# Experts' outputs of a mixture-of-experts layer: scatter to two tables in memory in place of a combine on TensorE

## The chip, the cores and the metric

One core of a Trainium2 chip runs the whole program. The metric is the device time of one execution in microseconds (us), lower is better. The three runs before the change have a median of 1986.42 us (1985.71 to 1988.87).

## What is computed

The program is a four-layer model on x of shape (8, 256, 128) float32, that is 2048 tokens of 128 channels. The change touches only the last stage, a mixture of experts. Reduced to what matters:

```python
p = softmax(router(layernorm(x)))             # (2048, 32)
top2 = the two largest of p for each token
for e in range(32):                           # each expert takes at most 80 tokens, by score
    rows = the 80 best-scored tokens that chose e
    h = silu(xe @ up_a[e]) * (xe @ up_b[e])   # 256 wide; plus a shared 128-wide part, times 0.05,
    y = h @ down[e]                           # whose weights two neighbouring experts share
    y = y * score / (sum of the token's two scores)
    moe[rows] += y
x_out = x + gate * moe
```

A token is in at most two experts' rows. Rows with score 0 fill an expert's 80 slots and count nothing.

## The kernel before, in words

Five engines run programs of their own and meet at barriers (`barrier`, L239). The attention and node layers ahead of the last stage take 1694 of 1995 us and are not touched.

The last stage (`moe_sp`, `moe_pool`, `moe_pe`, `moe_act`, `moe_dve`, L1725 to L2073) has three parts.

- Routing. VectorE normalises x into Qf and makes the tokens' statistics, TensorE and ScalarE the router, VectorE the two best experts of each token. SyncE stores the rows (Qf and one over the sum of a token's two scores) to the table s_rows in memory (L1743). Then VectorE takes each expert's 80 best tokens, eight at a time (L2000 to L2003). `slot` holds score and token number of each expert's 80 slots, `sloti` the number as an integer.
- The loop over 32 experts. POOL gathers 80 rows of s_rows into one of four buffers xg (L1764). TensorE transposes them (`turn`, L1811), ScalarE copies the result to xeT (L1901). TensorE multiplies with six 128-column weights (`up`, L1824, 80 columns of xeT each), ScalarE takes SiLU (L1905), VectorE makes the two parts of he (L2019, L2021), TensorE multiplies with the three second weights (`down`, L1835). VectorE scales y (L2035, L2041) and splits it into two parts of the fast matmul format (yb, L2043, L2045). VectorE also builds for each expert a one-hot matrix `sel` of 80 x 2048 (L2028), and TensorE adds y to the tokens' places by eight matmuls of 80 rows and 512 columns (`combine`, L1844); banks 0 to 3 gather all experts' sums. TensorE's order in a step is down(e), up(e+1), turn(e+2), combine(e). A gather waits until yb of four experts before is done (L1763). SyncE loads the weights of two experts (960 KB in four DMAs, L1737) into one of two buffers. First and last four experts are written out; the others are a hardware loop (`Fori`) of four.
- The end. VectorE copies four banks (L2064), TensorE transposes 16 blocks (L832), VectorE adds them, times the gate, onto X (L2070), SyncE stores 1 MB (L2077).

```python
            def step(e, u, par, first=False, left=4):
                down(e, u, par)
                if left > 1:
                    up(e + 1, (u + 1) % 4, ((u + 1) % 4) // 2)
                if left > 2:
                    turn(e + 2, (u + 2) % 4)
                combine(e, u, first, left == 1)
```

Of the kernel before, what the change touches and what calls it, by code (L numbers as in the profile page):

```python
# [140 lines left out]
def flamingo(nc, T, out):  # L141
    with ExitStack() as ctx:
# [1541 lines left out]
        iotaT = V[:, 0:NTOK]  # L1684
# [6 lines left out]
        XG = sb("XG", [P, NT, D + 1], scope=s5)  # L1691
# [4 lines left out]
        xg = sb("xg", [CAP, 4, D + 1], scope=s5)  # L1696
        xeT = sb("xeT", [P, 2, CAP], scope=s5)
        Wup = sb("Wup", [P, 2, 2, 512], scope=s5)
        Wdn = sb("Wdn", [P, 2, 2, 2, D], scope=s5)
        Aup = sb("Aup", [P, 2, 256], scope=s5)  # L1700
        Adn = sb("Adn", [P, 2, D], scope=s5)
        sil = sb("sil", [P, 2, 3, CAP], scope=s5)
        he = sb("he", [P, 2, 3, CAP], scope=s5)
        wsl = sb("wsl", [CAP, 2], scope=s5)
        ye = sb("ye", [CAP, 2, D], scope=s5)
        yb = sb("yb", [CAP, 2, 2, D], F32R, scope=s5)
        with ExitStack() as s6:
            sc = sb("sc", [E, 2, NTOK], scope=s6)
        sel = sb("sel", [CAP, 2, NTOK], F32R, scope=s5)
# [15 lines left out]
        def moe_sp(s):  # L1725
            e = s.eng
            for dst, src in moe_loads():
                e.dma_start(dst, src).then_inc(dma_in, 16)
            s.count("in", 6)

            def load_group(g, par):
                for dst, src in ((Wup[:, par], T["L3_upT"][ds(g, 1)].rearrange("a p e j -> p (a e) j")),
                                 (Wdn[:, par].rearrange("p e k c -> p (e k) c"),
                                  T["L3_downT"][ds(g, 1)].rearrange("a p x c -> p (a x) c")),
                                 (Aup[:, par], T["L3_aupT"][ds(g, 1)].rearrange("a p j -> p (a j)")),
                                 (Adn[:, par], T["L3_adnT"][ds(g, 1)].rearrange("a p j -> p (a j)"))):
# [10 lines left out]
            with e.Fori(0, (G - 2) // 2) as i:
                for par in range(2):

                    e.wait_ge(m_y_full, 2 * (2 * i + par + 1))  # L1750
                    load_group(2 * i + par + 2, par)
            s.barrier()
            s.barrier()

        def moe_pool(g):
# [4 lines left out]
            for k in range(E):  # L1760
                if k >= 4:

                    e.wait_ge(m_yb, 3 * (k - 3))  # L1763
# [3 lines left out]
            g.barrier()  # L1767
            g.barrier()

        def moe_pe(p):  # L1770
# [35 lines left out]
            def turn(e, u):  # L1806

                pe.wait_ge(m_g[u], 4 * (e - u) + 16)
                if not isinstance(e, int) or e >= 1:
                    pe.wait_ge(m_xt_free, e)  # L1810
                pe.transpose(bank[4][:, 0:CAP], xg[:, u, 0:D], ident[0:CAP, 0:CAP]).then_inc(m_xt_full, 1)  # L1811

            def up(e, u, par):

                q = u % 2
                if u % 2 == 0:
                    pe.wait_ge(m_w[par], 16 * (e - 2 * par) + 64)
                pe.wait_ge(m_xt_free, e + 1)
                o = bank[5 + q]

                for k in range(6):
                    w = (Wup[:, par, q, k * P:(k + 1) * P] if k < 2 else Aup[:, par, 0:P] if k == 2 else
                         Wup[:, par, q, (k - 1) * P:k * P] if k < 5 else Aup[:, par, P:2 * P])
                    last = pe.matmul(o[:, k * CAP:(k + 1) * CAP], w, xeT[:, q, :], start=True, stop=True,  # L1824
                                     skip_group_check=True)
                last.then_inc(m_up_full, 1)

            def down(e, u, par):
                q = u % 2
                pe.wait_ge(m_h, 2 * e + 2)  # L1830
                if not isinstance(e, int) or e >= 1:
                    pe.wait_ge(m_yb, 3 * e)
                for k in range(3):
                    w = Wdn[:, par, q, k] if k < 2 else Adn[:, par]
                    last = pe.matmul(bank[7][0:CAP, 0:D], he[:, q, k, :], w, start=(k == 0), stop=(k == 2))  # L1835
                last.then_inc(m_y_full, 1)

            def combine(e, u, first=False, end=False):
                q = u % 2
                pe.wait_ge(m_yb, 3 * e + 3)  # L1840
                pe.wait_ge(m_sel, e + 1)
                for c in range(4):
                    for k in range(2):
                        last = pe.matmul(bank[c][:, :], yb[:, q, k, :], sel[:, q, c * 512:(c + 1) * 512],  # L1844
                                         start=(first and k == 0), stop=(end and k == 1), skip_group_check=True)
                last.then_inc(m_comb, 1)

            def step(e, u, par, first=False, left=4):
                down(e, u, par)
                if left > 1:  # L1850
                    up(e + 1, (u + 1) % 4, ((u + 1) % 4) // 2)
                if left > 2:
                    turn(e + 2, (u + 2) % 4)
                combine(e, u, first, left == 1)
            turn(0, 0)
            up(0, 0, 0)
            turn(1, 1)
            for u in range(4):
                step(u, u, u // 2, first=(u == 0))
            with pe.Fori(1, E // 4 - 1) as i:  # L1860
                for u in range(4):
                    step(4 * i + u, u, u // 2)
            for u in range(4):
                step(E - 4 + u, u, u // 2, left=4 - u)
            p.barrier()
            transposes_pe(p, lambda t: xfT[:, t * P:(t + 1) * P], who="DDDD")
            p.barrier()

        def moe_act(a):
# [26 lines left out]
            def front(e, u):  # L1896
                q = u % 2
                act.wait_ge(m_xt_full, e + 1)
                if not isinstance(e, int) or e >= 2:
                    act.wait_ge(m_up_full, e - 1)  # L1900
                act.copy(xeT[:, q, :], bank[4][:, 0:CAP]).then_inc(m_xt_free, 1)  # L1901
                act.wait_ge(m_up_full, e + 1)
                if not isinstance(e, int) or e >= 2:
                    act.wait_ge(m_h, 2 * e - 2)
                act.activation(sil[:, q], bank[5 + q][:, 0:3 * CAP].rearrange("p (k s) -> p k s", k=3),  # L1905
                               ACT.Silu).then_inc(m_sil, 1)
            for u in range(4):
# [302 lines left out]
```

## Time and profile before

| | |
|---|---|
| median of three runs | 1986.42 us |
| the profiled execution's own time | 1996.73 us |
| its span, first to last instruction | 1994.8 us |
| last stage: first DMA issue of L1728 to the end | 1694.3 to 1994.8 us |
| TensorE busy | 1377.0 us (69%) |
| VectorE busy | 1362.2 us (68%) |
| ScalarE, POOL busy | 752.7 us, 410.0 us |
| granted clock of TensorE, mean | 0.852 of 2.4 GHz |

The profile is of one execution. Its own time is 10 us above the median of the unprofiled runs. Times in the rows count from the span's start. PE is the matmul side of TensorE, PEld its weight loads, DVE is VectorE, ACT ScalarE, SP SyncE; a "q" behind an engine's name marks its sequencer. A float32 matmul shows as two records.

### The profile page before, as it was taken

How to read it: one execution, taken by the hardware profiler on the slowest of the kernel's cores; microseconds unless marked ns; L12 is line 12 of the kernel's file. 1: busy time of each engine (PE TensorE's matmuls, PEld its weight loads, DVE VectorE, ACT ScalarE, POOL GpSimd, SP SyncE). 2: the span in 40 equal slices, each digit the busy share in tenths (PEclk: the TensorE clock that was granted, in tenths of full speed). 3: DMA queues.
4: the chain of work that ended last, by engine and by line, in shares of the span. 5: the costliest groups of instructions: out<-in, count | busy, mean ns of one | idle time of the engine just before them, and what ended most of it. 6: DMA issues, size and time to landing. Idle time of an engine off the chain costs nothing. (4 is left out here: it accounts for less than half of the span.)

```text
span 1994.8 us, 32063 instructions
## 1 busy us (share of the span) xinstructions
PE 1377.0 (69%) x12362; PEld 955.8 (48%) x12362; DVE 1362.2 (68%) x2054; ACT 752.7 (38%) x1092; POOL 410.0 (21%) x588
## 2 busy tenths in 40 slices
PE   0798189999999933888888834299514887120997
PEld 0565156666666621555665522166404454110897
DVE  5564457777777766676777778476587675869565
ACT  1255147667777731333333312145321365100110
POOL 6243232222222100222222200434102100000221
PEclk9898589999999975899999965589757799555899
DMA  2242322222232201000000000222001320110342
GB/s 69 49 68 35 92 81 88 83 89 89 85 91 85 89 24 41 1 1 1 1 1 1 1 11 0 48 60 53 12 0 32 65 50 19 61 21 0 93 146 86
DMA packets 115183, 95.88 MB, mean 48 GB/s; under 512 B 44180, under 2 KB 98516, under 8 KB 114132
## 3 DMA queue, kind: packets, MB, share of 16 engines
q1 hardware_dynamic: 114020, 92.63, 17.5%
q8 instruction: 96, 1.57, 0.3%
q0 software_dynamic: 1024, 1.32, 0.3%
q14 instruction: 43, 0.35, 0.1%
HBM read 33.23 MB, written 3.15 MB: 18 GB/s over the span
## 5 line engine op out<-in xcount | busy, mean ns | idle before, releaser
L586 ACT ACTIVATE Pt<-bank 128x1024 f32<-128x1024 f32 (+1 forms) x384 | 366.1, 953 | 181.0 <-PE bank L530 179.3
L642 DVE TENSOR_REDUCE l0f_Mf<-bank 128x4 f32<-128x1024 f32 x192 | 234.5, 1222 | 108.1 <-PE bank L509 108.0
L550 PE MATMUL bank<-Pt,V 128*32 128x256 f32 (+1 forms) x3072 | 199.0, 378 | 10.1 <-POOL Pt L391 8.9
L1102 POOL TENSOR_TENSOR Psum<-Pt 128x512 f32<-128x512 f32 x64 | 81.1, 1267 | 321.7 <-ACT Pt L1221 321.7
L550 PEld LDWEIGHTS bank<-Pt,V 128*32 128x32 f32 x3072 | 82.2, 112 | 82.8 <-issue 29.4
L832 PE MATMUL bank<-ident,Qf 128*128 128x128 f32 x64 | 14.1, 414 | 154.4 <-SPq L242 91.5
L391 POOL TENSOR_SCALAR_AFFINE_SELECT Pt<-Pt 128x512 f32<-128x512 f32 x128 | 81.5, 637 | 181.0 <-ACT Pt L586 181.0
L1269 DVE RECIPROCAL st<-bank 128x256 f32<-128x256 f32 x64 | 111.9, 1749 | 6.9 <-PE bank L1182 6.8
L1244 DVE TENSOR_TENSOR qk_lo<-bank,qk_hi 128x512 fp32r<-128x512 f32 x64 | 44.1, 689 | 103.2 <-ACT qk_hi L1213 103.2
L530 PE MATMUL bank<-l0f_QK 64*128 64x256 f32 x768 | 97.6, 333 | 19.8 <-DMA l0f_QK<-l0f_NMrow 19.2
L407 POOL CAST parts<-nodes 128x256 fp32r<-128x256 f32 x96 | 38.0, 396 | 305.1 <-PE bank L481 305.1
L642 DVE TENSOR_REDUCE l2x_Mf<-bank 128x4 f32<-128x1024 f32 x64 | 76.8, 1220 | 32.7 <-PE bank L509 32.7
L1764 POOL DMA_INDIRECT xg<-s_rows,sloti x32 | 29.3, 916 | 330.1 <-PEq L242 237.9
L1221 ACT ACTIVATE Pt<-bank 128x1024 f32<-128x1024 f32 x64 | 65.5, 1024 | 77.7 <-PE bank L1165 77.7
L530 PEld LDWEIGHTS bank<-l0f_QK 64*128 64x128 f32 x768 | 57.9, 187 | 73.2 <-ACT Pt L586 34.0
L832 PEld LDWEIGHTS bank<-ident,Qf 128*128 128x128 f32 x64 | 12.9, 224 | 155.3 <-SPq L242 92.2
L1177 PE MATMUL bank<-Pt,V 128*64 128x256 f32 x512 | 70.3, 395 | 19.6 <-DVE AnT L1271 19.6
L509 PE MATMUL bank<-l0f_QK 63*128 63x256 f32 x768 | 78.6, 283 | 5.8 <-DVE l0f_Mf L642 5.8
L1213 ACT CAST qk_hi<-bank 128x512 fp32r<-128x512 f32 x64 | 37.5, 586 | 115.0 <-PE bank L1121 115.0
L1248 DVE TENSOR_REDUCE Mx<-bank 128x4 f32<-128x1024 f32 x64 | 77.8, 1216 | 1.0 <-PE bank L1140 1.0
L590 ACT COPY OT<-bank 128x512 f32<-128x512 f32 x96 | 56.2, 586 | 54.6 <-PE bank L550 54.6
L559 PE MATMUL bank<-ident,OT 128*128 128x128 f32 x384 | 63.3, 289 | 13.0 <-ACT OT L590 5.5
(363 smaller groups left out, 3383.7 us busy)
## 6 DMA issues: line engine op xcount, KB each, us to landing
l0f_QK<-l0f_Z SPq DMA_DIRECT2D x288, 128.0 KB, 2.4
l2x_QK<-l2x_Z SPq DMA_DIRECT2D x96, 128.0 KB
Wup<-in_L_upT SPq DMA_DIRECT2D x16, 512.0 KB, 3.5
l0x_QK<-l0x_Z SPq DMA_DIRECT2D x48, 128.0 KB
Wdn<-in_L_downT SPq DMA_DIRECT2D x16, 256.0 KB, 3.6
Aup<-in_L_aupT SPq DMA_DIRECT2D x16, 128.0 KB, 3.5
l0f_QK<-l0f_NMrow SPq DMA_DIRECT2D x96, 4.0 KB
WeT<-in_L_WeT SPq DMA_DIRECT2D x1, 1280.0 KB
```

Source lines behind the costliest of these rows:

```text
L391: e.affine_select(diagonal, diagonal, [[0, 2], [0, 2], [1, P]], ALU.is_ge, 0.0, base=0, channel_multiplier=-1).then_inc(L.kept, 1)
L509: last = pe.matmul(bank[L.first(j) + x][:, t * S:t * S + w], L.QK[rs, u % L.ring, j, 0, t * P:(t + 1) * P], L.QK[rs, u % L.ring, j, 1, 0:w ...
L530: last = pe.matmul(bank[2 + x][:, t * S:t * S + S - q0], L.QK[rs, u % L.ring, j, 1, t * P:(t + 1) * P], L.QK[rs, u % L.ring, j, 0, q0:S], ...
L550: last = pe.matmul(bank[4][32 * x:32 * x + 32, o + q0:o + S], Va[:, 2 * n + k, 4 * j + x, :], Pp[:, (f + x // 2) % 4, x % 2, k * S:k * S + ...
L559: last = pe.transpose(b[:, (2 * t + k) * P:(2 * t + k + 1) * P], OT[:, k, t * P:(t + 1) * P], ident[:, :])
L586: act.activation(Pp[:, g % 4, :, 0:w], banks[:, 2:4, 0:w], ACT.Exp, scale=L.scale).then_inc(exp_done, 1)
L642: d.tensor_reduce(m, A.rearrange("p h (t k) -> p h t k", t=2), AX, ALU.max).then_inc(max_done, 1)
L1102: e.tensor_tensor(Psum[:, q % 2], Pp[:, q % 4, :, 0:S], Pp[:, q % 4, :, S:2 * S], ALU.add).then_inc(key_sum, 1)
L1177: pe.matmul(y[64 * x:64 * x + 64, 0:S], Vr[:, u % 8, k, 2 * j + x, :], Pp[:, g % 4, x, k * S:(k + 1) * S], start=(k == 0), stop=(k == 1), ...
L1221: act.activation(Pp[:, g % 4], banks[:, 2:4, :], ACT.Exp, scale=float(DH1) ** -0.5).then_inc(l1_exp, 1)
L1248: d.tensor_reduce(m[:, :, 2 * j:2 * j + 2].rearrange("p t h -> p h t"), banks[:, 0:2, :].rearrange("p h (t k) -> p h t k", t=2), AX, ALU.m ...
L1269: d.reciprocal(st1[:], y[:, S:2 * S]).then_inc(pair_done, 1)
```

## The change

Each expert's weighted rows are no longer added on TensorE. Two tables in memory, s_y_even and s_y_odd, have two rows for each token, one for its first and one for its second expert, and 160 rows that nobody reads. Both are filled with zeros at the stage's start (4 MB in two DMAs). VectorE works out a row number for each of the 80 slots (dsti), and POOL scatters ye (80 x 128) by it, into s_y_even for even experts and s_y_odd for odd ones. Scatter k waits for ye(k), and for the landing of scatter k-2 of the same table. Gather k+4 is issued behind scatter k. At the end SyncE waits for all scatters and reads both tables back (4 MB, eight DMAs with pieces of 1 KB), VectorE adds the four parts of each token and adds them times the gate onto X, in four chunks, and SyncE stores each chunk (256 KB).

With it: `combine`, `sel`, `yb`, the copies and transposes of the end go; TensorE's order in a step is turn(e+2), up(e+1), down(e), and down has two banks in turn; the loops of all engines are written out; the weights of two experts are one tensor of 960 KB and one DMA, with nine buffers in place of two, four of them in V; the load of a 1 MB iota goes; rows of s_rows are 130 floats wide in place of 129.

```diff
-        iotaT = V[:, 0:NTOK]
+        NW, WV = 9, 4
+        Wg = sb("Wg", [P, NW - WV, 1920], scope=s5)
...
+        Yl = V[:].rearrange("p (t a b c) -> p t a b c", t=NT, a=2, b=2)
...
         def moe_sp(s):
...
-            load_group(0, 0)
-            load_group(1, 1)
+            for y in ("s_y_even", "s_y_odd"):
+                e.dma_start(T[y][0:2 * NTOK].rearrange("(p r) c -> p (r c)", p=P),
+                            T["c_zero"].to_broadcast([P, 2 * NTOK * D // P])).then_inc(m_zero, 16)
+            for i in range(5):
+                e.dma_start(weights(i), T["L3_experts"][i]).then_inc(m_w[i], 16)
...
+            for i in range(NW, G):
+
+                e.wait_ge(m_y_full, 2 * (i - NW + 1))
+                e.dma_start(weights(i), T["L3_experts"][i]).then_inc(m_w[i % NW], 16)
+            for u in range(4):
+                e.wait_ge(m_put[u], 16 * (E // 4))
+            for c in range(4):
+                for b, y in enumerate(("s_y_even", "s_y_odd")):
+                    e.dma_start(Yl[:, 4 * c:4 * c + 4, b],
+                                T[y][1024 * c:1024 * (c + 1)].rearrange("(t p a) c -> p t a c", p=P, a=2)
+                                ).then_inc(m_fin[c], 16)
+            for c in range(4):
+                e.wait_ge(m_x, c + 1)
+                e.dma_start(out.rearrange("b (t p) c -> p (b t) c", p=P)[:, 4 * c:4 * c + 4],
+                            X[:, 4 * c:4 * c + 4]).then_inc(dma_out, 16)
...
         def moe_pool(g):
...
-            for k in range(E):
-                if k >= 4:
-
-                    e.wait_ge(m_yb, 3 * (k - 3))
+            for k in range(4):
+                gather(k)
+            for k in range(E):
+
+                e.wait_ge(m_rows, 2 * k + 2)
+                if k >= 2:
+                    e.wait_ge(m_put[(k - 2) % 4], 16 * ((k - 2) // 4 + 1))
+                e.indirect_dma_start(out=T["s_y_odd" if k % 2 else "s_y_even"],
+                                     out_offset=bass.IndirectOffsetOnAxis(ap=dsti[:, k % 4:k % 4 + 1], axis=0),
+                                     in_=ye[:, k % 4, :], in_offset=None).then_inc(m_put[k % 4], 16)
+                if k + 4 < E:
+                    gather(k + 4)
...
         def moe_pe(p):
...
+            turn(0)
+            turn(1)
+            up(0)
+            for e in range(E):
+                if e + 2 < E:
+                    turn(e + 2)
+                if e + 1 < E:
+                    up(e + 1)
+                down(e)
...
         def moe_dve(v):
...
+            v.link(d.tensor_scalar(dump[:], dump[:], 2.0, float(2 * NTOK), ALU.mult, ALU.add))
+            d.tensor_scalar(live[:], slot[:, 0], 0.0, None, ALU.is_gt)
+            v.link(d.tensor_scalar(rowS[:], slot[:, 1], 2.0, dump[:], ALU.mult, ALU.subtract))
+            v.link(d.tensor_tensor(rowS[:], rowS[:], live[:], ALU.mult))
+            v.link(d.tensor_scalar(rowS[:], rowS[:], dump[:], None, ALU.add))
...
+                d.scalar_tensor_tensor(out=dsti[:, u:u + 1], in0=xg[:, u, D + 1:D + 2], scalar=iotaE[0:CAP, e:e + 1],
+                                       in1=rowS[:, e:e + 1], op0=ALU.not_equal, op1=ALU.add).then_inc(m_rows, 1)
                 d.wait_ge(m_y_full, e + 1)
...
+                d.tensor_scalar(ye[:, u, :], bank[2 + e % 2][0:CAP, 0:D], xg[:, u, D:D + 1], slot[:, 0, e:e + 1],
+                                ALU.mult, ALU.mult).then_inc(m_rows, 1)
+            front(0)
+            for e in range(E):
+                if e + 1 < E:
+                    front(e + 1)
+                back(e)
...
             for c in range(4):
...
+                d.wait_ge(m_fin[c], 32)
+                two = Yl[:, 4 * c:4 * c + 4]
+                v.link(d.tensor_tensor(two[:, :, 0], two[:, :, 0], two[:, :, 1], ALU.add))
+                v.link(d.tensor_tensor(y, two[:, :, 0, 0], two[:, :, 0, 1], ALU.add))
+                d.scalar_tensor_tensor(out=x, in0=y, scalar=g, in1=x, op0=ALU.mult, op1=ALU.add).then_inc(m_x, 1)
```

How the steps stand on TensorE, in the middle of the loop, before (one step of the written-out experts; Wup, Wdn and Aup, Adn are an expert's own and the shared weights):

```order
L1835 MATMUL bank<-Wdn,he 80x128 x2
L1835 MATMUL bank<-Adn,he 80x128
L1824 MATMUL bank<-xeT,Wup 128x80 x2
L1824 MATMUL bank<-xeT,Aup 128x80
L1824 MATMUL bank<-xeT,Wup 128x80 x2
L1824 MATMUL bank<-xeT,Aup 128x80
L1811 MATMUL bank<-ident,xg 128x80
L1844 MATMUL bank<-sel,yb 128x512 x8
```

and after the change (two steps; Wg is the tile of the weights):

```order
L1834 MATMUL bank<-ident,xg 128x80
L1846 MATMUL bank<-xeT,Wg 128x80 x6
L1858 MATMUL bank<-Wg,he 80x128 x3
L1834 MATMUL bank<-ident,xg 128x80
L1846 MATMUL bank<-xeT,Wg 128x80 x6
L1858 MATMUL bank<-Wg,he 80x128 x3
```

The combine is gone, and the transpose of expert e+2, which waits for its gather, now stands ahead of up(e+1) and down(e).

On POOL, before, the loop is one row:

```order
L1764 DMA xg<-s_rows,sloti 80x129 x32
```

and after the change, from the loop's start:

```order
L1776 DMA xg<-s_rows,sloti 80x130 x4
L1786 DMA s_y_even<-ye,dsti 4256x128
L1776 DMA xg<-s_rows,sloti 80x130
L1786 DMA s_y_odd<-ye,dsti 4256x128
L1776 DMA xg<-s_rows,sloti 80x130
```

Gathers 0 to 3 still stand ahead; from then on each gather is issued behind a scatter that waits for ye.

## Rows read from the trace of the kernel before

**Rows 1.** Windows: length, busy us (count) by engine, granted clock, DMA share, GB/s.
```profile
1675.00:1685.00 10.00, 6.83 (x84) 3.59 (x88) 0.82 (x3) 6.73 (x7) 0.00 (x0) 1.00 0.01 2
1751.50:1755.50 4.00, 4.00 (x31) 4.00 (x30) 0.00 (x0) 1.02 (x1) 0.00 (x0) 0.79 0.00 0
1848.00:1856.00 8.00, 6.79 (x31) 6.58 (x32) 2.59 (x7) 1.94 (x4) 2.09 (x3) 0.50 0.06 13
1856.00:1859.80 3.80, 3.80 (x11) 2.95 (x11) 1.73 (x4) 0.49 (x2) 0.00 (x0) 0.50 0.04 11
1859.80:1863.00 3.20, 3.20 (x18) 3.20 (x16) 0.86 (x3) 0.00 (x0) 0.57 (x1) 0.50 0.22 42
1863.00:1980.00 117.00, 116.52 (x800) 105.06 (x799) 77.12 (x209) 15.13 (x59) 23.87 (x27) 1.00 0.39 126
```

**Rows 2.** Groups by line from 1840 us on: count, busy us, mean ns.
```profile
L1844 PE MATMUL bank<-sel,yb 80*128 80x512 f32 x256 | 68.5, 411 | 1.1 <-DVE yb L2045 1.1
L2028 DVE TENSOR_SCALAR sel<-V,slot 80x2048 fp32r<-80x2048 f32 x32 | 40.8, 1276 | 0.0
```

**Rows 3.** Timeline at 1.2 GHz, the loop's start: start us, us, instruction.
```profile
1853.31 0.98 PEld L1824 LDWEIGHTS bank<-xeT,Wup 128*128 128x128 f32 x4
...
1853.84 0.35 DVE L2041 TENSOR_SCALAR ye<-bank,wsl 80x128 f32<-80x128 f32 x1 [0.47 <-PE bank L1835]
...
1855.79 0.31 PEld L1811 LDWEIGHTS bank<-ident,xg 80*128 80x128 f32 x1
...
1856.25 0.37 ACT L1905 ACTIVATE sil<-bank 128x240 f32<-128x240 f32 x1 [4.59 <-PE bank L1824]
...
1859.64 1.06 PE L1835 MATMUL bank<-Wdn,he 128*80 128x128 f32 x4
```

**Rows 4.** Timeline at 2.4 GHz: one expert's step, and the last ye.
```profile
1971.48 0.53 PEld L1824 LDWEIGHTS bank<-xeT,Wup 128*128 128x128 f32 x4
...
1971.85 0.34 DVE L2041 TENSOR_SCALAR ye<-bank,wsl 80x128 f32<-80x128 f32 x1 [0.44 <-DVE wsl L2035]
...
1972.78 0.18 PEld L1811 LDWEIGHTS bank<-ident,xg 80*128 80x128 f32 x1
...
1973.81 0.23 DVE L2021 SCALAR_TENSOR_TENSOR he<-sil,bank 128x80 f32<-128x80 f32 x1
...
1975.76 0.35 DVE L2041 TENSOR_SCALAR ye<-bank,wsl 80x128 f32<-80x128 f32 x1 [0.46 <-DVE wsl L2035]
...
1979.62 0.35 DVE L2041 TENSOR_SCALAR ye<-bank,wsl 80x128 f32<-80x128 f32 x1 [0.40 <-DVE wsl L2035]
```

**Rows 5.** Timeline: a gather on POOL behind VectorE, and one behind another gather.
```profile
1847.37 0.91 POOL L1764 DMA_INDIRECT xg<-s_rows,sloti  x1 [0.30 <-issue]
...
1854.48 0.29 DVE L2045 TENSOR_TENSOR yb<-ye,yb 80x128 fp32r<-80x128 f32 x1
...
1855.04 0.91 POOL L1764 DMA_INDIRECT xg<-s_rows,sloti  x1 [5.55 <-DVE yb L2045]
```

**Rows 6.** The tile s_rows: its gathers from issue to landing.
```profile
DMA to landing us min/median/max: 2.3/2.6/5.0
```

**Rows 7.** Timeline, the end of the program.
```profile
1986.09 3.16 DVE L2070 SCALAR_TENSOR_TENSOR X<-bank,gates,X 128x512 f32<-128x512 f32 x4 [0.86 <-PE bank L832]
1989.32 0.41 SPq L2077 DMA_DIRECT2D x_out<-X  x1
```

**Rows 8.** Windows over DMAs: 512 B pieces in, weights (pieces of 2 to 4 KB), output (512 B).
```profile
4.00:5.50 1.50, 0.00 (x0) 0.00 (x0) 0.00 (x0) 0.00 (x0) 0.00 (x0) 1.00 1.06 321
1700.00:1705.00 5.00, 0.00 (x0) 0.00 (x0) 4.14 (x4) 0.62 (x1) 0.00 (x0) 0.50 1.01 401
1991.00:1994.00 3.00, 0.00 (x0) 0.00 (x0) 0.00 (x0) 0.00 (x0) 0.00 (x0) 0.50 1.01 284
```

**Rows 9.** Timeline: a wide and a small operation of VectorE.
```profile
1712.16 2.29 DVE L1925 TENSOR_TENSOR O<-Qf,st 128x2048 f32<-128x2048 f32 x1
...
1842.74 0.19 DVE L2004 TENSOR_SCALAR vals<-vals 32x80 f32<-32x80 f32 x1
```

More of the change, by code:

```diff
@@ L1743, in moe_sp @@
             e.dma_start(T["s_rows"].rearrange("(t p) c -> p t c", p=P), XG[:]).then_inc(xg_out, 16)
+            for i in range(5, NW):
+                e.dma_start(weights(i), T["L3_experts"][i]).then_inc(m_w[i], 16)
             e.wait_ge(xg_out, 16)
+            e.wait_ge(m_zero, 32)
             s.barrier()
             s.barrier()
[L1747 to L1752, printed above, removed]
+            for i in range(NW, G):
[12 more added lines that the diff above has]
+                            X[:, 4 * c:4 * c + 4]).then_inc(dma_out, 16)
+            s.count("out", 4)
             s.barrier()
@@ L1818, in up @@
+            def up(e):
+                q, g = e % 2, e // 2
+                w = weights(g)
+                pe.wait_ge(m_w[g % NW], 16 * (g // NW) + 16)
                 pe.wait_ge(m_xt_free, e + 1)
-                o = bank[5 + q]
+                if e >= 2:
+                    pe.wait_ge(m_h, 2 * e - 2)
                 for k in range(6):
[L1822 to L1825, printed above, removed]
+                    o = q * 512 + k * P if k < 2 else 1536 if k == 2 else q * 512 + (k - 1) * P if k < 5 else 1664
+                    last = pe.matmul(bank[5 + q][:, k * CAP:(k + 1) * CAP], w[:, o:o + P], xeT[:, q, :], start=True,
+                                     stop=True, skip_group_check=True)
@@ L1826, in up, with down @@
                 last.then_inc(m_up_full, 1)
-            def down(e, u, par):
-                q = u % 2
+            def down(e):
+                q = e % 2
+                w = weights(e // 2)
                 pe.wait_ge(m_h, 2 * e + 2)
-                if not isinstance(e, int) or e >= 1:
-                    pe.wait_ge(m_yb, 3 * e)
+                if e >= 2:
+                    pe.wait_ge(m_rows, 2 * e - 2)
                 for k in range(3):
-                    w = Wdn[:, par, q, k] if k < 2 else Adn[:, par]
-                    last = pe.matmul(bank[7][0:CAP, 0:D], he[:, q, k, :], w, start=(k == 0), stop=(k == 2))
+                    o = 1024 + q * 256 + k * P if k < 2 else 1792
+                    last = pe.matmul(bank[2 + q][0:CAP, 0:D], he[:, q, k, :], w[:, o:o + P], start=(k == 0),
+                                     stop=(k == 2))
@@ L1836, in down @@
                 last.then_inc(m_y_full, 1)
[L1838 to L1866, printed above, removed]
+            turn(0)
[7 more added lines that the diff above has]
+                down(e)
             p.barrier()
@@ L2047, in step @@
-            def step(e, u, end=False):
-                back(e, u)
-                if not end:
-                    front(e + 1, (u + 1) % 4)
-                    choose(e + 1, (u + 1) % 4)
-            front(0, 0)
-            choose(0, 0)
-            for u in range(4):
-                step(u, u)
-            with d.Fori(1, E // 4 - 1) as i:
-                for u in range(4):
-                    step(4 * i + u, u)
-            for u in range(4):
-                step(E - 4 + u, u, end=(u == 3))
@@ L2073, in moe_dve @@
             v.barrier()
         def finish_sp(s):
-            s.eng.dma_start(out.rearrange("b (t p) c -> p (b t) c", p=P), X[:]).then_inc(dma_out, 16)
-            s.eng.wait_ge(dma_out, 16 * s.count("out", 1))
+            s.eng.wait_ge(dma_out, 16 * s.count("out", 0))
         block = ctx.enter_context(nc.Block())
```

129 lines of the change are left out of this document (49 added, 80 removed).

## The prediction

> **What bounds the kernel now.** First the windows. From 1863 to 1980 us PE is busy 116.52 of 117.00 us at the full clock, VectorE 77 us: the loop is bound by TensorE [rows 1]. Then the groups by line: of that time the combine, L1844, is the largest part, 68.5 us or 2.14 us an expert [rows 2]. Then the timeline, for the pace: ye starts at 1971.85 and 1975.76, so an expert takes 3.91 us; the last ye ends at 1979.97, the first at 1854.19 [rows 3, 4]. The end is serial: behind the last ye come combine, copies, transposes, the addition to X and a store, 14.8 us to the span's end at 1994.8 [rows 4, 7]. The sum below goes against this execution, whose own time, 1996.73 us, is 10.3 us above the median of 1986.42; I carry the difference over to the median. A measurement can tell about 0.2%, 4 us, from no change.
>
> **Ahead of the loop: +1 us.** Four linked small operations and a fifth make the row numbers before POOL may start, at 0.19 us and a gap each [rows 9]: 1.0 us, on the path. The zeros (4.2 MB) and weights (4.9 MB) are asked for at 1694 and on; at the 400 GB/s of the weights' window that is 23 us, even at half of it 46 us, and nobody needs them before the loop, 150 us later [rows 8]. Nothing for them; if the cover were gone it would be seen at the s_rows store. The weights in the loop come nine buffers ahead, also nothing.
>
> **The loop: a new wait.** The combine and `sel` go. What is left on PE for an expert, by the starts of weight loads: at 2.4 GHz up 1.30 us (1971.48 to 1972.78), down and turn 0.8 more, 2.1 together [rows 4]; at 1.2 GHz up 2.48 us (1853.31 to 1855.79), down 1.3 (four of its six records 1.06, less overlap) and turn 0.2, 4.0 together [rows 3]. But PE waits. Gather k+4 stands behind scatter k, scatter k behind ye(k); on PE turn(k+4) stands ahead of up(k+3) and down(k+2), which ye(k+2) needs. So two experts cost one round:
> - ye to POOL's start 0.27 us (1854.77 to 1855.04) [rows 5];
> - the scatter on POOL 0.91 + 0.30 [rows 5]. No row shows a scatter; the gather, 80 pieces of 516 B, is nearest, and I take it. Nothing at all is the lower end, twice it the upper;
> - the gather to its landing 2.6, from 2.3 to 5.0 [rows 6];
> - turn and its start 0.3;
> - up(k+3) to ye(k+2). VectorE makes he(k+3) ahead of ye(k+2). At 2.4 GHz from 1971.48 to 1974.04 for he, then dsti 0.15 and ye 0.35: 3.1 us [rows 4]. At 1.2 GHz up and down take 3.8 on PE, some 0.2 to finish, ye 0.35: 4.4 us [rows 3].
>
> Sums: 7.5 us a pair at 2.4 GHz, 8.8 at 1.2 GHz, or **3.7 and 4.4 us an expert**, against 3.91 now. So the clock decides the sign.
>
> **The clock.** PE begins the loop at 1.2 GHz. From 1848 to 1856 it does turns, ups and downs, is busy 6.79 of 8.00 us, the last three throughout, and the clock stays low; it rises at 1863.0, behind the first combine (1856 to 1859.8), a down and an up [rows 1]. In the router's matmuls, 1751.5 to 1755.5, it falls (0.79 on average) while PE is busy 4.00 of 4.00 us [rows 1]. The new loop consists of just the turns, ups and downs that ran eight microseconds at the low level here, with PE waiting 0.4 us an expert besides. I take it that the clock stays at 1.2 GHz for about two thirds of the loop, and that where it rises, the waits (PE then busy 2.1 of 3.7 us) bring it back down in part. Against that: at 1675 to 1685 it holds 1.00 with PE busy 6.83 of 10 us [rows 1]. The Trainium skill (TensorE: Matmul & The Clock Gate, "What's actually happening") says that the throttled state is the default and that the clock is set by how busy PE has recently been; read as busy time, that rule would raise the clock after the first experts, which is the rival below; the rows from 1848 to 1856 do not agree with that reading.
>
> The loop in numbers: ye(0) moves from 1854.2 to 1857.2 (1.0 ahead, turn(2) and up(1) now before down(0), 2.9, less 0.9 us in which PE stood idle), ye(1) follows at 1861.3 (PE's 4.0). Then 28 experts to ye(29): two thirds at 4.4 and a third at 3.7, 116.7 us: 1978.0. The last two need no gather: 4.5 us. ye(31) ends at 1982.5, against 1980.0: **+2.5 us**. All at 1.2 GHz: 1861.3 + 123.2 + 5.2 = 1989.7, +9.7. All at 2.4 GHz from ye(1) on: 1861.3 + 103.6 + 2.9 = 1967.8, -12.2.
>
> **The end: +7 us.** From the last ye: POOL 0.3, the scatter's landing 2.6 (as a gather), SyncE's issue to first data 1.1. Then 4.2 MB in pieces of 1 KB: the windows show 321/1.06 = 303 GB/s for 512 B and some 400 for larger pieces [rows 8]; I take 365, 11.5 us, from 10.5 to 13.9. A receipt 0.4. VectorE then adds the last chunk: half of 2.29, a quarter and a bit (0.69), and 0.75: 2.7 us with links [rows 7, 9]; the other chunks go beside the reads. SyncE's last store, 256 KB: issue to data 1.0, 0.9 at 284 GB/s, landing and end 0.9: 2.8 us [rows 7, 8]. Together 21.4, against 14.8: **+6.6 us**, from +5 to +10. The Trainium skill (DMA: Bandwidth & Descriptors, "Anatomy of one DMA") fits 2.0 us plus bytes over 436 GB/s; by that the reads would take 11.6 us with their start, 1 us less than my 12.6 to the same point.
>
> **Sum:** +2.5 + 6.6 = +9.1 us (the 1 us ahead is in ye(0)), or 1986.4 + 9.1 = 1995.5 us. The removed work is large (68 us of matmuls), and the gain is lost to a low clock, the round through POOL, and 4 MB read where nothing hides it.
>
> **Rivals.**
> 1. The clock rises after the first few experts and holds (the other side: faster). From the point where it rises each expert costs 3.7; with at most four experts at 4.4 the loop ends 9 to 12 us earlier, and with the end's +6.6 the sum is -6 to -3: 1981 to 1984. For it: 68% busy held the clock at 1675. It decides from about half of the loop at 2.4 GHz: below that the sum is above the 4 us.
> 2. The clock stays at 1.2 GHz for the whole loop: +9.7 + 6.6 = +16.3, 2003. For it: the rows from 1848 to 1856.
> 3. The scatters cost more, on POOL or by making the gathers land later, say 3.0 in place of 2.6 us and twice the time on POOL: 0.8 us more an expert, 22 over 28 of them, on top of rival 2 some 2025. For it: gathers landed as late as 5.0 us beside the weights' traffic. Against: the median is 2.6 there, and POOL has time.
> 4. The round is shorter than I count (scatter nearly free, landings of 2.3): 0.7 us less an expert at 2.4 GHz, PE's 2.1 not yet the bound: about 1960 to 1972. This needs the clock as well.
>
> **How the numbers follow.** Forecast (mixed clock, +4 to +13) 0.38; rival 1 0.24; rival 2 0.20; rival 3 0.05; rival 4 0.07; a rise near the loop's middle, within 4 us either way, 0.06. Of rival 1 0.15 lies below -4 us and 0.09 within 4; of the forecast 0.04 lies within 4. Faster: 0.15 + 0.07 = 0.22. Same: 0.09 + 0.04 + 0.06 = 0.19. Slower: 0.34 + 0.20 + 0.05 = 0.59. The forecast's own range is 1990 to 2000. The range takes in rival 1 with an end of +5 and rival 2 with one of +10, and leaves out rival 3 and most of rival 4: 1977 to 2007.
>
> **What would show it.** Granted clock in the windows of the new loop: mostly 0.50 by the forecast, 1.00 by rival 1. The distance of two ye: 4.4 us at 0.50 and 3.7 at 1.00; PE's idle time before the turn ended by the gather's landing, and POOL's before the scatter by ye. From the last ye to the end 21.4 us, with DMA near 1.0 and 365 GB/s for 11 us of it. Wrong it would be if PE ran its experts without idle time, if the clock rose in the first 15 us, if a scatter cost POOL 2 us, or if the reads at the end began before the last scatter landed.

## Result and the profile after

The changed kernel takes 2005.99 us (median of 5 runs, 1996.80 to 2009.37), the kernel before in the same call 1988.64 us (5 runs, 1985.71 to 1990.93). The ratio is **1.0074, 95% interval 1.0047 to 1.0102**: slower by some 15 us, where the forecast was slower by 9.1 us.

The two profiled executions have the same length by chance (1996.80 and 1996.73 us), because in that of before the untouched stages took 14 us more: its last stage begins at 1694.3 us, that of after at 1680.4. So I compare the last stage alone, from its first DMA issue (L1728 before, L1734 after), in three pieces cut at the ends of the first and the last ye:

| us | before | forecast | after |
|---|---|---|---|
| stage's start to ye(0) | 159.9 | 162.9 | 162.6 |
| ye(0) to ye(31) | 125.8 | 125.3 | 129.1 |
| ye(31) to the end | 14.9 | 21.4 | 22.9 |
| whole stage | 300.5 | 309.6 | 314.6 |
| granted clock from ye(0) to ye(31) | 0.96 | | 0.72 |

The stage is 14.1 us longer, which agrees with the medians (17 us) and the ratio's interval (9 to 20 us). Of the 14.1 us, 2.7 lie ahead of ye(0), 3.3 in the loop and 8.0 in the end. Each piece is from one execution: that of after is the fastest of its five and has a mean clock of 0.846, where the three slowest have 0.831 to 0.839, and in the run "even table only" below, whose loop is the same, the middle piece is 132.6 us. A difference of less than some 4 us between two loops therefore shows nothing. Every table entry is a difference of rows like these, the timeline of after (start us, us, instruction) at the stage's start, ye(0), ye(31) and the last scatter:

```profile
1680.39 0.33 SPq L1734 DMA_DIRECT2D r<-in_L_r1T  x1
...
1842.55 0.41 DVE L2038 TENSOR_SCALAR ye<-bank,xg,slot 80x128 f32<-80x128 f32 x1 [0.27 <-PE bank L1858]
...
1971.64 0.41 DVE L2038 TENSOR_SCALAR ye<-bank,xg,slot 80x128 f32<-80x128 f32 x1 [0.40 <-issue]
1972.61 0.92 POOL L1786 DMA_INDIRECT s_y_odd<-ye,dsti  x1 [0.30 <-issue]
1974.84 0.38 SPq L1759 DMA_DIRECT2D V<-s_y_even  x1
...
1980.39 1.23 DVE L2050 TENSOR_TENSOR V<-V 128x1024 f32<-128x1024 f32 x1 [8.35 <-DMA V<-s_y_odd]
...
1989.30 1.22 DVE L2050 TENSOR_TENSOR V<-V 128x1024 f32<-128x1024 f32 x1 [0.18 <-DMA V<-s_y_odd]
```

**Windows over the loop** of after (length, busy us and count of PE, PEld, VectorE, ScalarE, POOL, then granted clock, DMA share, GB/s), the answer to [rows 1]:

```profile
1842.00:1849.00 7.00, 2.58 (x22) 2.35 (x20) 1.61 (x8) 0.60 (x2) 3.71 (x4) 0.97 0.47 161
1849.00:1855.00 6.00, 5.40 (x26) 5.40 (x27) 1.00 (x4) 0.82 (x3) 0.44 (x1) 0.52 0.02 5
1855.00:1865.00 10.00, 9.03 (x43) 8.28 (x43) 2.00 (x8) 1.20 (x4) 4.73 (x6) 0.50 0.35 119
1865.00:1875.00 10.00, 7.73 (x38) 7.36 (x37) 2.00 (x8) 1.20 (x4) 4.05 (x5) 0.50 0.36 120
1875.00:1885.00 10.00, 8.54 (x41) 8.16 (x41) 2.00 (x8) 1.20 (x4) 3.68 (x4) 0.50 0.33 111
1885.00:1900.00 15.00, 12.84 (x69) 12.24 (x68) 3.92 (x16) 2.16 (x7) 5.55 (x7) 0.60 0.39 125
1900.00:1920.00 20.00, 12.32 (x79) 11.87 (x80) 3.84 (x16) 2.39 (x8) 7.84 (x9) 0.83 0.25 86
1920.00:1935.00 15.00, 10.52 (x77) 9.84 (x76) 3.75 (x16) 2.39 (x8) 7.80 (x9) 0.87 0.09 23
1935.00:1950.00 15.00, 14.59 (x76) 13.88 (x75) 3.27 (x13) 2.39 (x8) 5.96 (x7) 0.56 0.09 21
1950.00:1960.00 10.00, 5.62 (x48) 5.15 (x48) 2.55 (x12) 1.42 (x5) 5.95 (x7) 1.00 0.11 25
1960.00:1972.00 12.00, 8.71 (x74) 7.79 (x73) 4.15 (x18) 1.94 (x6) 4.38 (x6) 1.00 0.07 17
```

Where before had PE busy throughout at 1.00, here the clock is 0.50 from 1849 to 1897 with shorter spells later (the longest 1934.5 to 1948.2), and PE is idle for 44% of the time from 1950 to 1960, where the clock is 1.00 (busy 5.62 of 10), and for 27% of the next 12 us. The weights' traffic, 111 to 125 GB/s from 1855 to 1900, lies on the first half.

**Groups by line**, after, 1840 to 1973 us (count | busy, mean ns | idle time before, what ended it):

```profile
L1776 POOL DMA_INDIRECT xg<-s_rows,sloti x28 | 25.5, 910 | 8.5 <-issue 8.5
L1786 POOL DMA_INDIRECT s_y_even<-ye,dsti x16 | 14.9, 932 | 29.3 <-DVE ye L2038 26.2 <-issue 2.1 <-DVE dsti L2035 1.0
L1786 POOL DMA_INDIRECT s_y_odd<-ye,dsti x16 | 14.9, 931 | 43.9 <-DVE ye L2038 43.3 <-issue 0.6
L1834 PE MATMUL bank<-ident,xg 80*128 80x80 f32 x29 | 9.7, 334 | 31.4 <-DMA xg<-s_rows,sloti 31.0 <-DVE he L2024 0.4
```

This is the new wait: PE before the transpose, ended by the gather's landing, 31 us; POOL before the scatter, ended by ye. The combine (68.5 us, [rows 2]) is gone.

**One round of two experts at 2.4 GHz**, timeline of after:

```profile
1952.02 0.29 PE L1834 MATMUL bank<-ident,xg 80*128 80x80 f32 x1 [2.01 <-DMA xg<-s_rows,sloti]
...
1953.50 0.82 PE L1858 MATMUL bank<-V,he 128*80 128x128 f32 x6
...
1954.62 0.40 DVE L2038 TENSOR_SCALAR ye<-bank,xg,slot 80x128 f32<-80x128 f32 x1
...
1955.30 0.93 POOL L1786 DMA_INDIRECT s_y_odd<-ye,dsti  x1 [2.16 <-DVE ye L2038]
...
1956.54 0.91 POOL L1776 DMA_INDIRECT xg<-s_rows,sloti  x1 [0.30 <-issue]
...
1958.98 0.14 PEld L1834 LDWEIGHTS bank<-ident,xg 80*128 80x128 f32 x1 [2.27 <-DMA xg<-s_rows,sloti]
```

From the transpose at 1952.02 to the end of ye 3.0 us, to POOL 0.28, scatter 0.93 and 0.31, the gather's issue to the next transpose but one 2.44: 6.96 us for two experts, 3.5 each.

**Beside the weights** the same wait is longer. A weights' DMA is issued at 1867.28; the gather issued at 1869.21 lets PE go at 1873.49, 4.28 us later:

```profile
1867.28 0.33 SPq L1754 DMA_DIRECT2D V<-in_L_experts  x1
...
1869.21 0.91 POOL L1776 DMA_INDIRECT xg<-s_rows,sloti  x1 [0.30 <-issue]
...
1873.49 0.40 PE L1834 MATMUL bank<-ident,xg 80*128 80x80 f32 x1 [2.27 <-DMA xg<-s_rows,sloti]
```

The kernel before had this too, but no one waited for it: its gather of 1862.4 lands after 4.0 us beside weights, its gather of 1867.3 after 2.3 us without. The traffic of the two stretches, windows of before:

```profile
1863.00:1867.00 4.00, 4.00 (x29) 3.63 (x29) 2.57 (x7) 0.49 (x2) 0.33 (x1) 1.00 0.62 226
1867.00:1871.00 4.00, 4.00 (x30) 3.61 (x30) 2.60 (x8) 0.49 (x2) 0.91 (x1) 1.00 0.03 10
```

**The end** of after, windows over the reads:

```profile
1977.00:1980.00 3.00, 0.00 (x0) 0.00 (x0) 0.00 (x0) 0.00 (x0) 0.00 (x0) 0.50 1.08 365
1980.00:1985.00 5.00, 0.00 (x0) 0.00 (x0) 4.27 (x5) 0.00 (x0) 0.00 (x0) 0.50 1.10 350
1985.00:1990.00 5.00, 0.00 (x0) 0.00 (x0) 4.44 (x6) 0.00 (x0) 0.00 (x0) 0.50 1.08 337
```

### The profile page after: what moved, and what is told of

Its sections match the earlier page's. It is cut to its first block and busy times, and to the rows that moved or that the text cites. A ratio compares the mean times of both kernels' runs of the same rounds, so it can differ in the third digit from the quotient of the medians.

```text
span 1995.0 us, 31005 instructions
## 1 busy us (share of the span) xinstructions
PE 1328.9 (67%) x12090; PEld 922.1 (46%) x12090; DVE 1315.5 (66%) x1968; ACT 756.0 (38%) x1092; POOL 444.8 (22%) x620
## 3 DMA queue, kind: packets, MB, share of 16 engines
q0 software_dynamic: 2048, 2.65, 0.5%
## 5 line engine op out<-in xcount | busy, mean ns | idle before, releaser
L642 DVE TENSOR_REDUCE l0f_Mf<-bank 128x4 f32<-128x1024 f32 x192 | 234.5, 1221 | 109.2 <-PE bank L509 109.2
L642 DVE TENSOR_REDUCE l2x_Mf<-bank 128x4 f32<-128x1024 f32 x64 | 76.8, 1219 | 32.8 <-PE bank L509 32.7
L2024 DVE TENSOR_TENSOR he<-sil,bank 128x160 f32<-128x160 f32 x32 | 10.3, 321 | 104.8 <-ACT sil L1911 91.9
```

The source lines that it names most:

```text
L642: d.tensor_reduce(m, A.rearrange("p h (t k) -> p h t k", t=2), AX, ALU.max).then_inc(max_done, 1)
```

## Experiments

Theory: the loop is paced by the round of two experts through POOL and the gather's landing; the low clock and the weights' traffic lengthen it; the wide matmuls of the combine had held the clock up. Rivals: the clock or the weights cost nothing by themselves; written-out code costs time. "Clock" in the table is the mean granted clock from ye(0) to ye(31). Eleven kernels ran. Distances are those of the table above, from the profiled execution; ratios are against the kernel before in the same call. The medians of before were 1989.11 us for the first four runs, 1989.14 for the next four, 1987.57 for the last three.

| run | us | ratio (95%) | to ye(0) | ye(0) to ye(31) | to the end | clock |
|---|---|---|---|---|---|---|
| no weights in the loop | 1989.20 | 0.9996 (0.9973 to 1.0018) | 162.4 | 113.7 | 23.1 | 0.82 |
| eight gather buffers | 1968.47 | 0.9889 (0.9860 to 0.9918) | 162.8 | 93.5 | 22.9 | 0.82 |
| a wide matmul | 1986.88 | 0.9985 (0.9972 to 0.9997) | 162.6 | 109.2 | 22.9 | 1.00 |
| even table only | 2000.49 | 1.0054 (1.0037 to 1.0070) | 162.4 | 132.6 | 20.2 | 0.73 |
| before, no combine | 2004.12 | 1.0081 (1.0055 to 1.0107) | 159.9 | 136.5 | 13.5 | 0.65 |
| before, written out | 1992.65 | 1.0011 (0.9989 to 1.0032) | 159.9 | 125.6 | 15.4 | 0.96 |
| eight buffers, wide | 1971.52 | 0.9925 (0.9905 to 0.9944) | 163.8 | 95.0 | 22.5 | 1.00 |
| gather first | 1985.23 | 0.9981 (0.9963 to 1.0000) | 162.6 | 112.1 | 23.6 | 0.80 |
| eight, one table | 1972.90 | 0.9926 (0.9900 to 0.9952) | 168.2 | 95.7 | 23.9 | 0.89 |
| eight, one table, warm | 1972.98 | 0.9930 (0.9903 to 0.9956) | 162.8 | 98.2 | 23.2 | 0.97 |
| eight, no weights | 1964.64 | 0.9896 (0.9864 to 0.9928) | 162.8 | 87.4 | 22.8 | 0.88 |

### The weights in the loop

```diff
-            for i in range(NW, G):
-                e.wait_ge(m_y_full, 2 * (i - NW + 1))
-                e.dma_start(weights(i), T["L3_experts"][i]).then_inc(m_w[i % NW], 16)
...
-                pe.wait_ge(m_w[g % NW], 16 * (g // NW) + 16)
+                pe.wait_ge(m_w[g % NW], 16)
```

> The changed kernel without the seven weight loads that fall in the loop (experts 18 to 31 use weights of earlier experts: that part of the result is left wrong; every instruction but the loads stays). Theory A (weights' traffic makes the gathers land late, and in the new loop TensorE waits for them): first to last ye falls from 129 us to 118 us or less, since the rounds of two experts before 1900 us shrink from 9.4 to 8.8 us or, at 2.4 GHz, to 7.0; median 2006 to about 1996. Rival (the clock alone, or the scatters' place ahead of the gathers, makes the round): 126 us or more, median within 3 us of 2006.

Measured: 129.1 falls to 113.7 us. In this run a gather at the same place takes the usual time although the clock is 0.50; timeline:

```profile
1867.50 0.91 POOL L1772 DMA_INDIRECT xg<-s_rows,sloti  x1 [0.30 <-issue]
...
1869.99 0.40 PE L1830 MATMUL bank<-ident,xg 80*128 80x80 f32 x1 [0.55 <-DMA xg<-s_rows,sloti]
```

2.49 us instead of 4.28. The seven loads, all of them in time, cost 15 us in all. Not all of it comes straight from the delayed gathers: the clock rose from 0.72 to 0.82, so 41 us of this loop were at the low level instead of 72. An estimate from this run's own rounds (two experts take 6.9 to 7.2 us at 1.00 and 8.5 to 8.7 at 0.50): 31 us less at the low level are some 3.6 rounds at 1.4 us, 5 us. That leaves some 10 us for the gathers. Whether the late gathers themselves bring the clock down isn't shown.

### The length of the round

```diff
-        xg = sb("xg", [CAP, 4, D + 2], scope=s5)
+        xg = sb("xg", [CAP, 8, D + 2], scope=s5)
```
(and gather k+8 in place of k+4 behind scatter k)

> The changed kernel with eight gather buffers in place of four, so that gather k+8 stands behind scatter k. Theory (the round ye, scatter, gather, turn, up, down sets the pace): TensorE no longer waits for a gather after the first; the pace falls to TensorE's own, 4.0 us an expert at 1.2 GHz, or to POOL's 2.4 us at 2.4 GHz; first to last ye from 129 us to 80 us where the clock rises early, to 120 us where it never does; median 1960 to 1995. Rival (scatters or their DMA queue set the pace: scatter k waits for scatter k-2): first to last ye stays at 125 us or more, with POOL waiting for a landing.

Measured: 93.5 us, 36 less than with four buffers (the clock rose too, from 0.72 to 0.82). PE's idle time before the transpose, groups by line, 1848 to 1960 us, with eight buffers:

```profile
L1835 PE MATMUL bank<-ident,xg 80*128 80x80 f32 x30 | 8.2, 275 | 1.5 <-issue 1.5
```

No gather is waited for any more. The total is 1.1% under the kernel before: **with this the change pays.**

The other way to shorten the round is the order on POOL:

```diff
                 e.wait_ge(m_rows, 2 * k + 2)
+                if k + 4 < E:
+                    gather(k + 4)
                 if k >= 2:
                     e.wait_ge(m_put[(k - 2) % 4], 16 * ((k - 2) // 4 + 1))
...
-                if k + 4 < E:
-                    gather(k + 4)
```

> The changed kernel with gather k+4 issued ahead of scatter k, still in four buffers: the scatter's 1.2 us on POOL leave the round of two experts, and so does the wait for scatter k-2 to land. Theory: 1.2 us less for each of 14 to 15 rounds, 17 us, perhaps some of it taken back where another thing binds: from the first ye to the last 129 falls to 110 to 116 us, the total to about 1988. Rival (gathers land late beside the weights' traffic, and that alone sets the pace): less than 8 us.

Measured: 112.1 us, 17.0 less, as forecast, but in part by luck. Two ye of this run, two experts apart, at 1.00 and without a load beside:

```profile
1924.24 0.41 DVE L2038 TENSOR_SCALAR ye<-bank,xg,slot 80x128 f32<-80x128 f32 x1 [0.47 <-PE bank L1858]
...
1930.65 0.41 DVE L2038 TENSOR_SCALAR ye<-bank,xg,slot 80x128 f32<-80x128 f32 x1 [0.51 <-PE bank L1858]
```

Such rounds take 5.6 to 6.5 us here and mostly 6.9 to 7.0 in after: 0.4 to 1.4 us less, where 1.2 was forecast for each. The rest comes with the clock, 0.80 instead of 0.72 (45 us at the low level instead of 72). That the scatter's place in the queue was on the path of the pairs holds.

### The clock

```diff
                 down(e)
+                if e < E:
+                    pe.matmul(bank[0][:, :], ident[:, :], Qf[:, 0:4, :], start=True, stop=True, skip_group_check=True)
```

> The changed kernel with one more matmul behind each down: 128 rows, 128 columns of ident, 512 columns of Qf, into a bank that nobody reads. It costs TensorE 1.7 us at 1.2 GHz and 0.85 us at 2.4 GHz an expert. Theory (the removed combine had kept the clock high): the clock rises within the first four experts and stays 1.00 to the loop's end; a round stays near 7.0 to 7.6 us, since the matmul fits the wait for the gather; first to last ye 129 us to 115 us, median about 1995. Rival (the clock is not what costs, or the matmul only adds): first to last ye 135 us or more, or clock below 0.9 in the loop.

Measured: clock 1.00 from ye(0) to ye(31), 109.2 us, though 64 records, 32.8 us busy, were added to PE's work. The reverse, on the kernel before:

```diff
-                for c in range(4):
-                    for k in range(2):
-                        last = pe.matmul(bank[c][:, :], yb[:, q, k, :], sel[:, q, c * 512:(c + 1) * 512],
-                                         start=(first and k == 0), stop=(end and k == 1), skip_group_check=True)
-                last.then_inc(m_comb, 1)
+                pe.matmul(bank[0][:, 0:32], yb[:, q, 0, :], sel[:, q, 0:32], start=first, stop=end,
+                          skip_group_check=True).then_inc(m_comb, 1)
...
-                d.tensor_copy(xfT[:, c * 512:(c + 1) * 512], bank[c][:, :])
+                d.tensor_copy(xfT[:, c * 512:(c + 1) * 512], bank[0][:, 0:32].unsqueeze(1).to_broadcast([P, 16, 32]))
```

> The kernel before with the eight 512-column matmuls of the combine cut to one of 32 columns, so that the tokens' sums are left out; gathers, weights, sel and yb stay. Theory (the wide matmuls of the combine kept TensorE at 2.4 GHz): the loop falls to 1.2 GHz for a good part, and the distance from the first ye to the last, 126 us before, falls by 10 to 45 us only, to 80 to 115 us, although 66 us of matmuls are gone. Rival (the clock needs no wide matmuls; only the new round through POOL made TensorE idle): the clock stays at 2.4 GHz, and the distance is what VectorE or the gathers allow at that clock, 65 to 75 us.

Measured: slower than with the combine. 125.8 us became 136.5, above even the theory's 115. Windows:

```profile
1851.00:1945.00 94.00, 78.58 (x369) 76.72 (x369) 46.88 (x127) 9.10 (x36) 17.18 (x19) 0.50 0.31 102
1950.00:1985.00 35.00, 26.98 (x218) 24.61 (x216) 27.78 (x75) 5.40 (x21) 7.23 (x8) 1.00 0.40 136
```

For 94 us PE is busy 84% of the time, at the low level throughout, and an expert takes 5.2 us. Near 1945 the clock rises and the same code takes 3.3 us an expert. Against it the run without weights has PE busy 35.74 of 51 us, 70%, at a clock of 0.90:

```profile
1849.00:1900.00 51.00, 35.74 (x263) 32.61 (x262) 13.01 (x56) 8.11 (x27) 25.13 (x28) 0.90 0.09 23
```

So PE's busy share alone doesn't set the clock; the wide matmuls do keep it up, shown both ways. What brings the new loop of short matmuls down or up isn't shown. In after two experts ran at 2.4 GHz, then the first late gather (5.0 us of PE's idle time, until 1849.60) was followed by 48 us at the low level; without the loads the clock stayed at 1.00 for 20 us and then fell all the same, for 10 us.

### Written-out code

The kernel before with its four hardware loops replaced by written-out ones.

> The kernel before with its four hardware loops written out, nothing else. Rival (written-out code costs time by itself: several engines stand still together for 1 to 3 us, with nothing that the profile shows, in the runs of the changed kernel): the distance from the first ye to the last grows from 126 us by 5 us or more, and idle time before instructions put down to issue appears on ACT and VectorE. Theory (the changed kernel's loop is long by the round through POOL, the weights' traffic and the clock alone): no difference, within 2 us.

Measured: 125.6 against 125.8 us. At the pace of the kernel before, 3.9 us an expert, written-out loops cost nothing. The changed kernel with hardware loops was not tried.

### Round and clock together

> Eight gather buffers and one matmul of 512 columns, thrown away, behind each down: the round through POOL is longer than two experts need, and the clock stays. Theory: both losses go, the clock is 1.00 in the loop, an expert takes what TensorE needs, 2.1 + 0.9 us, so from the first ye to the last 90 to 97 us, no better than the 93.5 us of eight buffers alone (what the clock gives, the added matmul takes). Rival (waits for the round and low clock are one loss, and the gathers' landings beside the weights still bind): above 100 us.

Measured: 95.0 us at a clock of 1.00, as the theory said: with eight buffers the clock gives what the added matmul takes. But clean steps are 2.93 us (91 for the 31 from ye(0) to ye(31)), and stretches of some 6 us lie between them. They show in the last run too:

> Eight gather buffers, and no weights loaded in the loop (experts 18 to 31 use other experts' weights). Theory (with eight buffers the gathers' landings are covered, so the weights' traffic costs the loop nothing): 93.5 stays within 3 us. Rival (beside weights' loads ACT, VectorE and PE stand still together for 1 to 3 us whatever the gathers do): the distance falls by 8 us or more, and idle time put down to issue or remote goes.

Measured: 93.5 falls to 87.4 us, between theory (within 3) and rival (8 or more): neither holds. The clock is 0.88 instead of 0.82, and the stops stay, so the loads don't make them. One is seen in the timeline of the run with eight buffers:

```profile
1857.79 1.50 PE L1847 MATMUL bank<-xeT,V 128*128 128x80 f32 x12
...
1860.39 0.23 ACT L1904 COPY xeT<-bank 128x80 f32<-128x80 f32 x1 [2.52 <-remote]
...
1863.29 0.37 ACT L1912 ACTIVATE sil<-bank 128x240 f32<-128x240 f32 x1 [2.68 <-PE bank L1847]
```

The twelve records are up of one expert. They end at 1859.3, and ScalarE begins the SiLU that waits for them 4.0 us later; its own copy ahead of that is 2.5 us late too. The two kernels of before and the changed one with four buffers have no such late SiLU. It happens only in the five runs with eight buffers, with the weights and without, at either clock. Its cause **stays open**. The loading of code is a rival that no run tests in this loop; the profile's two instruction queues have six packets from ye(0) to ye(31) with eight buffers and six with four, so their number doesn't tell.

### The end

```diff
-                for b, y in enumerate(("s_y_even", "s_y_odd")):
+                for b, y in enumerate(("s_y_even",)):
...
-                d.wait_ge(m_fin[c], 32)
+                d.wait_ge(m_fin[c], 16)
```

> The changed kernel, reading back only the table of even experts (odd experts' part of the result is left out; the additions stay). Theory (the end is bound by 4.2 MB of reads at 350 GB/s): the stretch from the last ye to the end falls by 2.1 MB or 5.5 to 6 us from 23.0 us, until VectorE's 2.7 us a chunk bounds it: 17 to 18 us. Rival (latency of the last scatter and of the stores makes the end): it falls by less than 3 us. The loop is unchanged; median 2000 with the loop's scatter of some us.

Measured: from ye(31) to the end 20.2, 2.7 less with half of the bytes. The theory's 17 to 18 fails, and the number is the rival's (less than 3), but not its reason. VectorE is what remains; its timeline in this run:

```profile
1987.65 1.22 DVE L2050 TENSOR_TENSOR V<-V 128x1024 f32<-128x1024 f32 x1 [6.65 <-DMA V<-s_y_even]
...
1990.30 1.22 DVE L2050 TENSOR_TENSOR V<-V 128x1024 f32<-128x1024 f32 x1
...
1995.60 1.22 DVE L2050 TENSOR_TENSOR V<-V 128x1024 f32<-128x1024 f32 x1
```

Four chunks at 2.65 us, the last three without a wait: the additions are nearly as long as the reads of 4.2 MB, whose chunks come 2.98 us apart in after (1980.39 and 1983.37). Halving one alone uncovers the other. So both were halved, in a kernel with eight buffers:

```diff
-                if k >= 2:
-                    e.wait_ge(m_put[(k - 2) % 4], 16 * ((k - 2) // 4 + 1))
-                e.indirect_dma_start(out=T["s_y_odd" if k % 2 else "s_y_even"],
+                if k >= 1:
+                    e.wait_ge(m_put[(k - 1) % 4], 16 * ((k - 1) // 4 + 1))
+                e.indirect_dma_start(out=T["s_y_even"],
...
-                v.link(d.tensor_tensor(two[:, :, 0], two[:, :, 0], two[:, :, 1], ALU.add))
```
(and the odd table's zeros and reads go)

> Eight gather buffers, and one table in place of two (a token's two rows never meet, so one table holds both): half the zeros, half the reads at the end, one addition of VectorE less; each scatter now waits for the one before it to land. Theory (the end is 4.2 MB read at 340 GB/s, then VectorE's additions): from the last ye to the end 22.9 falls to 14 to 16.5 us; the loop stays at eight buffers' 93.5 us, up to 6 us more if a scatter lands later than 2.6 us, since POOL's scatter, gather and wait are then 3 us an expert. Total about 1961. Rival (the end is latencies in a row, as the even table alone, 20.2 us, could suggest): 18 us or more.

Measured: 23.9 us, no gain, but not by the rival's reason. Timeline of the last scatters:

```profile
1946.75 0.92 POOL L1787 DMA_INDIRECT s_y_even<-ye,dsti  x1 [2.00 <-DVE ye L2040]
1949.64 0.92 POOL L1787 DMA_INDIRECT s_y_even<-ye,dsti  x1 [1.98 <-DMA s_y_even<-ye,dsti]
1952.55 0.92 POOL L1787 DMA_INDIRECT s_y_even<-ye,dsti  x1 [1.99 <-DMA s_y_even<-ye,dsti]
1955.45 0.92 POOL L1787 DMA_INDIRECT s_y_even<-ye,dsti  x1 [1.99 <-DMA s_y_even<-ye,dsti]
1957.66 2.03 SPq L1760 DMA_DIRECT2D V<-s_y_even  x4
```

From the reads' issue at 1957.66 to the end at 1970.5 it takes 12.8 us, where after takes 20.2 (1974.84 to 1995.0): the end itself did fall by 7.3 us. A scatter that waits for the one before it, though, takes 2.90 us, PE ran ahead of it by three experts, and that queue (8.7 us behind 1946.75) gave the gain back. That the way to ye(0) is 5.4 us longer in this one run (168.2) comes from the clock in the router's matmuls, 53 us into the stage. It fell to the low level 7 us earlier there than in the run with eight buffers alone; windows at the same distance from the stage's start, this run first:

```profile
1735.50:1742.50 7.00, 6.66 (x8) 0.86 (x6) 0.00 (x0) 1.00 (x3) 0.00 (x0) 0.50 0.00 0
1744.50:1751.50 7.00, 6.32 (x33) 3.43 (x31) 0.00 (x0) 2.55 (x4) 0.00 (x0) 0.98 0.00 0
```

The router's code is the same in both, so the 5.4 us are not an effect of the table; in the next run, with the same table, the way is 162.8. The wait was added because two scatters to one table may otherwise be under way together; without it, it wasn't tried.

> As the one with eight buffers and one table, with a matmul of 256 columns, thrown away, behind each down (0.5 us an expert). Theory: the clock stays at 1.00 as with 512 columns, PE needs 2.6 us an expert, from the first ye to the last 84 to 92 us against 93.5 with a clock of 0.82; the end as with one table. Total 1955 to 1960. Rival (half the columns don't hold the clock): clock at 0.85 or less and 93 us or more.

Measured: clock 0.97, so the rival fell, but 98.2 us, outside the theory's 84 to 92: POOL's scatter takes 2.90 us an expert and paces parts of the loop, and the stops above are in it. The total, 1972.98 us, is 13 to 18 above the forecast. Of the kernels that leave nothing out, the one with eight buffers alone has the lowest ratio, 0.9889 of before; its interval overlaps those of the other three with eight buffers (0.9925 to 0.9930), so that it is the best of them isn't shown.

## Why the prediction was right

The sign, and the reason that the combine's 68 us would not come back, held. The size held less well: 17 us measured (medians), 14.1 us between the two profiled executions, 9.1 forecast, and 2005.99 us lies above the forecast's own 1990 to 2000, near rival 2's 2003 and at the upper end of the range that was given. By its steps:

- **Ahead of the loop, ye(0) 3 us later: right.** Measured 2.7 us.
- **The round of two experts: right in kind and in most of its size.** Forecast 0.27 + 1.21 + 2.6 + 0.3 + 3.1 = 7.5 us at 2.4 GHz; measured 6.96. The scatter on POOL, priced by the gather's 0.91 + 0.30, measured 0.93 + 0.30. The landing was 2.44, not 2.6, and transpose to ye 3.0, not 3.4. Eight buffers (36 us less) and the other order on POOL (17 us less) show that this round set the pace.
- **"The weights in the loop come nine buffers ahead, also nothing": this term failed.** It asked whether the weights would be late; what counts is whom they hold up. The sum took the gathers' landing at 2.6 us, the median of [rows 6], although the row's upper end of 5.0 belonged to just such stretches. With the loads taken out the loop is 15.4 us shorter, some 10 by the gathers and 5 by the clock on the estimate above. That is also rival 3's mechanism (gathers that land later), given 0.05: it said 3.0 us, and the gathers beside the seven loads, all in the first half of the loop, landed as late as 4.3 to 5.1. Rival 3's other half, twice the time on POOL, did not come: a scatter took 0.93 us.
- **The clock: right that the wide matmuls kept it and that the new loop would lose part of it.** Forecast two thirds of the loop at 1.2 GHz. Measured 0.72 on average, 56% of it at the low level. One detail was wrong: "if the clock rose in the first 15 us" stood among the signs against the forecast, and the first two experts did run at 2.4 GHz (0.97 from 1842 to 1849) until the first late gather. At 1.2 GHz away from the weights (1934.5 to 1948.2) four ye in a row stand 5.8, 4.0 and 4.6 us apart: 9.8 and 8.6 us for two, against 8.8 forecast.
- **The loop's total is right partly by luck:** 125.3 forecast, 129.1 measured. Less time at the low level and a shorter round took off what the weights added.
- **The end, 21.4 forecast, 22.9 measured.** The whole 1.5 us is in the reads: from their first issue (1974.84) to VectorE's start on the last chunk (1989.30) 14.5 us, against 12.6 and 0.4 for the receipt, 13.0. The sum took 365 GB/s throughout; the windows show 365 at first, then 350 and 337. That the other chunks' additions lie beside the reads holds, but by 0.3 us a chunk only.
- Rival 1 (the clock holds after the first experts) and rival 4 fell: the clock was 0.50 for 48 us in a row. Rival 2 (1.2 GHz throughout) fell too, though its 2003 us is the nearest number: 44% of the loop was at 2.4 GHz.

The Trainium skill (TensorE: Matmul & The Clock Gate, "What's actually happening") says that the clock is set by how busy PE has recently been. Read as the share of time in which PE is busy, that is contradicted here by two rows, 84% busy at 0.50 and 70% busy at 0.90. The Trainium skill (DMA: Bandwidth & Descriptors, "Anatomy of one DMA") fits one DMA issued by GpSimd with 2.0 us plus bytes over 436 GB/s. The prediction used that fit for eight reads issued by SyncE, an estimate of 11.6 us; the trace has the 14.5 us above, so it doesn't carry over.

## What to carry to other kernels

When work leaves a busy engine, ask which ring of waits now sets the pace: here it was four buffers, a queue with a scatter ahead of the next gather, and a landing. Double the buffers before judging such a change: the same change went from 0.7% slower to 1.1% faster than before. A transfer that is always in time can still be dear, by the small transfers that wait beside it; and wide matmuls that hold TensorE's clock may be worth more than the time they take, so that taking them out alone can lose (136.5 against 125.8 us).

## What was not expected

- Taking the combine's 68.5 us of matmuls from the kernel before, and adding 10.7 us of narrow ones, made its loop 10.7 us longer, with PE 84% busy for 94 us at 1.2 GHz.
- A gather of 80 pieces of some 500 B lands 3.8 to 5.1 us behind its issue beside a weights' load of 1 MB, and 2.3 to 2.5 without.
- With eight buffers ScalarE starts up to 4 us after the matmul that it waits for, again and again, and nothing read from the profile says why.
